# Big-head attention on one core: accumulators over three banks, queries in the score ring, diagonal subtractions on GpSimd

## The reference, cut to what matters

```python
qkv = jnp.einsum('bnc,fc->bnf', xn, w_qkv)                 # 8 heads x 128
q = q * scale_attn
sim = jnp.einsum('bihd,bjhd->bhij', q, k)
sim = jnp.where(causal_mask, neg, sim)
attn = jax.nn.softmax(sim, axis=-1)
out = jnp.einsum('bhij,bjhd->bihd', attn, v)
out = jnp.einsum('bnf,cf->bnc', out.reshape(b, n, 1024), w_out)
x = _layernorm(x + out)                                    # then the next block's own norm
```

## Time and profile before

| | |
|---|---|
| median of 3 runs | 2038.41 us (2037.45 to 2038.93) |
| profiled execution, its own time | 2044.93 us |
| span from its first to its last instruction | 2043.2 us |
| TensorE busy, share of the span | 1804.0 us, 88% |
| VectorE busy | 1570.7 us, 77% |
| ScalarE busy | 1374.6 us, 67% |
| GpSimd busy | 423.4 us, 21% |
| mean granted TensorE clock | 0.925 |

### The profile page before, as it was taken

The page is one execution under the profiler, slowest core; times in us unless marked ns, Lnnn a source line. Parts: engine busy times, 40 slices in busy tenths (PEclk is TensorE's granted clock), DMA queues, the critical chain, the costliest instruction groups (busy, mean ns, idle before and its releaser), DMA issues. The chain is left out here.

```text
span 2043.2 us, 40577 instructions
## 1 busy us (share of the span) xinstructions
PE 1804.0 (88%) x15880; PEld 967.7 (47%) x15880; DVE 1570.7 (77%) x2299; ACT 1374.6 (67%) x2569; POOL 423.4 (21%) x650
## 2 busy tenths in 40 slices
PE   6799999999999798669889998989678999999784
PEld 2122222222223388536778887978512322233384
DVE  5899999999997443457878788877578979886534
ACT  3499999999999543246555556565347898888431
POOL 4201000000002314323332221222231101122413
PEclk8599999999999989879999999989867999999698
DMA  5000000000000268400000000000100000000274
GB/s 168 1 3 3 4 11 4 5 9 4 7 8 7 96 226 297 154 4 1 1 1 1 1 1 1 1 1 1 54 0 2 4 4 12 5 12 6 60 263 153
DMA packets 52879, 81.57 MB, mean 40 GB/s; under 512 B 9200, under 2 KB 37744, under 8 KB 52560
## 3 DMA queue, kind: packets, MB, share of 16 engines
q1 hardware_dynamic: 47520, 70.50, 10.8%
q0 software_dynamic: 3072, 6.30, 1.0%
q10 hardware_dynamic: 2096, 2.17, 0.4%
HBM read 64.13 MB, written 12.06 MB: 37 GB/s over the span
## 5 line engine op out<-in xcount | busy, mean ns | idle before, releaser
L827 DVE TENSOR_REDUCE a_mx<-psum 128x2 f32<-128x1024 f32 (+2 forms) x832 | 906.3, 1156 | 77.0 <-PE psum L602 42.2
L753 ACT ACTIVATE a_cs<-psum 128x512 f32<-128x512 f32 (+3 forms) x1664 | 857.0, 572 | 78.6 <-PE psum L620 60.1
L643 PE MATMUL psum<-a_cs,a_V 128*16 128x256 f32 (+1 forms) x6400 | 501.6, 385 | 20.8 <-ACT a_OD L733 9.7
L602 PE MATMUL psum<-a_KS,a_QS 48*128 48x512 bf16 (+3 forms) x1664 | 330.2, 389 | 29.9 <-DVE a_mx L827 27.7
L620 PE MATMUL psum<-a_QS,a_KS 51*128 51x512 bf16 (+3 forms) x1664 | 336.7, 379 | 4.9 <-ACT a_cs L753 3.1
L2140 PE MATMUL psum<-b_VW,b_ST 128*128 128x129 f32 x2176 | 256.3, 279 | 21.1 <-DVE X L2265 21.1
L2140 PEld LDWEIGHTS psum<-b_VW,b_ST 128*128 128x128 f32 x2176 | 250.4, 195 | 23.1 <-DVE X L2265 23.1
L620 PEld LDWEIGHTS psum<-a_QS,a_KS 51*128 51x128 bf16 x1664 | 87.8, 93 | 354.4 <-ACT a_cs L753 310.3
L643 PEld LDWEIGHTS psum<-a_cs,a_V 128*16 128x16 f32 x6400 | 107.5, 94 | 244.2 <-issue 120.3
L2240 DVE TENSOR_TENSOR b_M<-b_M,b_ST 128x512 f32<-128x512 f32 (+3 forms) x288 | 174.8, 607 | 37.6 <-ACT b_ST L2179 6.7
L2186 ACT ACTIVATE b_ST<-b_ST 128x2048 f32<-128x2048 f32 x48 | 91.9, 1914 | 153.3 <-DVE b_ST L2248 153.3
(11 more groups left out here) (232 smaller groups left out, 1776.7 us busy)
## 6 DMA issues: line engine op xcount, KB each, us to landing
e_W<-in_l_experts SPq DMA_DIRECT2D x45, 576.0 KB, 5.5
e_W<-in_l_experts SPq DMA_DIRECT2D x21, 768.0 KB, 5.8
yg<-e_yout SPq DMA_DIRECT2D x14, 256.0 KB, 5.8
xg<-zeros SPq DMA_DIRECT2D x2, 1472.0 KB, 10.1
a_cs<-in_rope ACTq DMA_DIRECT2D x4, 512.0 KB, 10.5
a_QS<-a_mrow SPq DMA_DIRECT2D x128, 3.0 KB
a_cs<-in_rope SPq DMA_DIRECT2D x1, 2048.0 KB, 8.1
a_num<-a_OD SPq DMA_DIRECT2D x120, 16.0 KB
```

The costliest lines, as they stand in the source:

```text
L602: mm = pe.matmul(ps[:, 2 * slot + half, 0:width], QS[rows, 2 * p + i, q_cols(qb, qt * P, P)], KS[rows, 2 * p + i, c * BLK:c * BLK + width] ...
L643: mm = pe.matmul(ps[32 * j:32 * j + 2 * HD, AV_BANK, a:b], V[:, kt, HPP * p + j, :], probs(e, a, b), start=(kt == 0 and half == 0), stop=last,
L753: act.activation(probs(HPP * s + j, c, BLK), ps[:, plan.bank(entry), c:BLK], ACT.Exp, scale=scale).then_inc(exp_done, 1)
L827: dve.tensor_reduce(mx[:, pk % 2, qt, 2 * i:2 * i + 2, c], banks, AX.X, ALU.max).then_inc(max_done, 1)
```

## The change

Four things change in `big_head_attention` and its planner.

The two accumulators take turns over three banks (5, 6 and 7), so a product waits for the accumulation three halves back instead of two. Value products use three banks as well. Queries and folds lose their own bank and take their places in the ring of the five score banks, in the order in which TensorE makes queries, scores and folds. The four diagonal subtractions of an atom move from VectorE to GpSimd, into its list at the event `subtract`. The early folds, and the third `normalize`, are placed later on the plan's clock.

```diff
@@ KeyPlan.turn
-                self.norms += [(self.clock + 0.5 + n, ("measure", g, behind)), (self.clock + 12.0 + 2 * n + 2 * (n // 2), ("normalize", g)),
-                               (self.clock + 17.0 + 3 * n, ("fold", g))]
+                self.norms += [(self.clock + 0.5 + n, ("measure", g, behind)), (self.clock + (12.0, 14.0, 47.0)[n], ("normalize", g)),
+                               (self.clock + (45.0, 48.0, 54.0)[n], ("fold", g))]
@@ KeyPlan.lay
+        self.ring = [event for event in self.events if event[0] in ("query", "score", "fold")]
+        self.place_of = {event: n for n, event in enumerate(self.ring)}
@@ big_head_attention
-    S_BANKS, G_BANK, O_BANK = 5, 5, 6
+    RING, O_BANK, O_BANKS = 5, 5, 3
...
+        def o_bank(a, half):
+            return O_BANK + (2 * a + half) % O_BANKS
+        def bank_of(event):
+            return plan.place_of[event] % RING
+        def wait_bank(eng, event):
+            n = plan.place_of[event] - RING
+            if n < 0:
+                return
+            what, of = plan.ring[n][:2]
+            if what == "query":
+                eng.wait_ge(g_done, of + 1)
+            elif what == "fold":
+                eng.wait_ge(norm.h_ready, early[of] + 1)
+            else:
+                eng.wait_ge(copied, plan.tile0[of] + plan.ring[n][2] + 1)
@@ gpsimd
+                def subtract(a):
+                    pool.wait_ge(row_done, a + 1)
+                    for i in range(TPB):
+                        one = tile(a, TPB * plan.atoms[a][0] + i)
+                        pool.tensor_tensor(one, one, row[:, a % 2, i * P:], ALU.subtract).then_inc(diag_sub, 1)
...
+                    elif event[0] == "subtract":
+                        subtract(event[1])
@@ tensor, product
-                        elif a:
-                            pe.wait_ge(added, 2 * a - 1 + half)
+                        elif 2 * a + half >= O_BANKS:
+                            pe.wait_ge(added, 2 * a + half - O_BANKS + 1)
@@ vector, subtract
-                    for i in range(TPB):
-                        one = tile(a, TPB * qb + i)
-                        dve.tensor_tensor(one, one, row[:, a % 2, i * P:], ALU.subtract).then_inc(diag_sub, 1)
```

More of the change, by code:

```diff
@@ L2039, in v_bank @@
         def v_bank(n):
-            return O_BANK + n % 2
+            return O_BANK + n % O_BANKS
+        def o_bank(a, half):
[13 more added lines that the diff above has]
+                eng.wait_ge(copied, plan.tile0[of] + plan.ring[n][2] + 1)
         def x_cols(g):
@@ L2083, in _ @@
             def _(pe):
-                asked, folded = [0], [0]
                 def fold(g):
[L2087 to L2091, removed]
+                    wait_bank(pe, ("fold", g))
+                    norm.transpose(pe, early[g], bank_of(("fold", g)))
                 def query(a):
                     qb, h = plan.atoms[a]
[L2095 to L2100, removed]
+                    wait_bank(pe, ("query", a))
+                    pe.matmul(ps[:, bank_of(("query", a)), :], A[:, h, :], xnT[:, qb * BLK:(qb + 1) * BLK],
                               start=True, stop=True).then_inc(g_ready, 1)
@@ L2104, in value @@
                     n = 2 * t + c
-                    if n >= 2:
-                        pe.wait_ge(v_a if n % 2 == 0 else v_d, n // 2)
+                    if n >= O_BANKS:
+                        pe.wait_ge((v_a, v_d)[(n - O_BANKS) % 2], (n - O_BANKS) // 2 + 1)
                     pe.matmul(ps[:, v_bank(n), :], xnT[:, t * P:(t + 1) * P],
@@ L2111, in score @@
                 def score(a, kt):
-                    n, c = plan.tile0[a] + kt, plan.first_col(a, kt)
+                    c = plan.first_col(a, kt)
                     if kt == 0:
@@ L2116, in score @@
                         pe.wait_ge(x_low, kt // TPB + 1)
-                    if n >= S_BANKS:
-                        pe.wait_ge(copied, n - S_BANKS + 1)
-                    keys, out_ = slice(kt * P, (kt + 1) * P), ps[:, n % S_BANKS, c:BLK]
+                    wait_bank(pe, ("score", a, kt))
+                    keys, out_ = slice(kt * P, (kt + 1) * P), ps[:, bank_of(("score", a, kt)), c:BLK]
                     pe.matmul(out_, xL[:, keys], GH[:, a % 2, c:BLK], start=True, stop=False)
@@ L2139, in product @@
                         cols = slice((i % 2) * W, (i % 2 + 1) * W)
-                        mm = pe.matmul(ps[:, O_BANK + half, cols], ST[:, plan.at[a][kt // TPB], kt % TPB, i * P:(i + 1) * P],
+                        mm = pe.matmul(ps[:, o_bank(a, half), cols], ST[:, plan.at[a][kt // TPB], kt % TPB, i * P:(i + 1) * P],
                                        VW[:, kt, h, :], start=(kt == 0 and i % 2 == 0), stop=(kt == TPB * qb + i),
@@ L2163, in query @@
                         act.wait_ge(s_ready, plan.tile0[a - 1])
-                    act.activation(GH[:, a % 2, :], ps[:, G_BANK, :], ACT.Copy).then_inc(g_high, 1)
+                    act.activation(GH[:, a % 2, :], ps[:, bank_of(("query", a)), :], ACT.Copy).then_inc(g_high, 1)
                 def split(g):
@@ L2178, in score @@
                         act.wait_ge(av_done, 2 * (plan.before[a] + 1))
-                    act.activation(tile(a, kt), ps[:, n % S_BANKS, c:BLK], ACT.Copy).then_inc(copied, 1)
+                    act.activation(tile(a, kt), ps[:, bank_of(("score", a, kt)), c:BLK], ACT.Copy).then_inc(copied, 1)
                 def exponentials(a):
@@ L2204, in _ @@
                     elif event[0] == "fold":
-                        norm.store(act, early[event[1]], event[1], G_BANK)
+                        norm.store(act, early[event[1]], event[1], bank_of(event))
                         norm.keep(act, early[event[1]], event[1])
@@ L2213, in query @@
                     dve.wait_ge(g_high, a + 1)
-                    dve.tensor_tensor(GL[:, a % 2, :], ps[:, G_BANK, :], GH[:, a % 2, :].bitcast(F32),
+                    dve.tensor_tensor(GL[:, a % 2, :], ps[:, bank_of(("query", a)), :], GH[:, a % 2, :].bitcast(F32),
                                       ALU.subtract).then_inc(g_done, 1)
@@ L2259, in accumulate @@
                     mine = rec[:, a % 2, 2 * half:2 * half + 2]
-                    sums = ps[:, O_BANK + half, 0:2 * W].rearrange("p (i n) -> p i n", n=W)[:, :, P:W]
+                    sums = ps[:, o_bank(a, half), 0:2 * W].rearrange("p (i n) -> p i n", n=W)[:, :, P:W]
                     dve.reciprocal(mine.rearrange("p (i o) -> p i o", o=1), sums).then_inc(inverted, 1)
@@ L2264, in accumulate @@
                         t = TPB * qb + 2 * half + i
-                        ins = dve.scalar_tensor_tensor(out=X[:, t, :], in0=ps[:, O_BANK + half, i * W:i * W + P],
+                        ins = dve.scalar_tensor_tensor(out=X[:, t, :], in0=ps[:, o_bank(a, half), i * W:i * W + P],
                                                        scalar=mine[:, i:i + 1], in1=X[:, t, :], op0=ALU.mult, op1=ALU.add)
```

## The result

The changed kernel takes **2248.91 us** (median of 4 runs, 2246.83 to 2251.89) where the kernel before took 2037.93 on the same chip (4 runs, 2035.38 to 2038.93): a ratio of 1.1038, 95% interval 1.1019 to 1.1058. It is 10% slower; forecast were 2226 us and a range of 2170 to 2295. The profiled execution took 2247.01 us with a span of 2245.2, GpSimd's busy time went from 423.4 to 510.0 us, VectorE's from 1570.7 to 1516.9, and the mean granted clock from 0.925 to 0.888.

The account below looks back on a forecast made before the run. The stage was taken as a loop through ScalarE, VectorE and GpSimd, lengthened by GpSimd's reconfigurations: 50 + 29 + 57 + 31 + 20 - 6 - 3 + 10 = +188 on 2044.9, 2233, less 6.5: 2226 us, range 2170 to 2295.

Parts of the forecast that it names:

- atoms 0, 1, 2 and 15: Single atoms: 13.6 us for atom 15, 7 each for atoms 1 and 2, 3 for atom 0; together +31.
- six pairs: Pairs of atoms in blocks 1 and 0: a round of 29.0 us instead of 19.5, +9.5 each, +57.
- block 2: Rounds of atoms 17 to 23: 26.4 us instead of 19.29, +7.1 each, +50; nothing counted for atom 16.
- block 3 without 27, and the folds: Seven rounds of 28.8 us instead of 24.68, +29; moved folds end TensorE's 7.6 us stall, less 2: -6.
- atom 27: Subtractions queued behind the powers and `call` reduction: 30.1 us from its reduction to its exponentials instead of 13.4; +20.
- TensorE's clock: Longer idle in block 2 lowers the granted clock, slowing score tiles; VectorE's chain hides most: +10, bounds 0 and 40.
- T: GpSimd's reconfiguration from a reduction to a tensor_tensor, ahead of the subtractions: 6.7 to 6.9 us, taken as 6.9.
- R: GpSimd's reconfiguration from a tensor_tensor back to a reduction, behind the masks: 5.6 to 5.9 us, taken as 5.9.
- R without cover: Rival: reconfiguration issued only after the instruction's own wait, so short idle times don't hide it: +36, 2262 us; chance 0.11.
- the ring: Queries among the score banks let TensorE run four tiles ahead, not five: nothing, or 0.7 us a round without cover.
- the prediction's own sign of being wrong: The forecast is wrong if something else, such as TensorE at half clock, makes rounds longer than 30 us.
- The blocking rival: Rival: reconfigurations cost nothing, but GpSimd's and VectorE's subtractions block each other: +28 less 22, 2044 us; chance 0.04.

Follow-up runs that it names:

- e3: The changed kernel with the subtractions back on VectorE and, in their place on GpSimd, a tiny multiplication nobody reads; 2144.98 us, ratio 1.0497 to before.
- e4: The changed kernel with one more all-reduce, of a buffer nobody reads, directly behind each run of subtractions on GpSimd; 2175.19 us, ratio 1.0653 to before.
- e1: The changed kernel with only the diagonal subtractions put back on VectorE; 2029.17 us, ratio 0.9929 to before.
- e7: The changed kernel with extra matmuls ahead of each fourth score tile in blocks 2 and 3, keeping TensorE busy; 2235.15 us, ratio 1.0951 to before.
- e2: The kernel before with only the diagonal subtractions moved to GpSimd; 2250.77 us, ratio 1.1018 to before.
- e8: The kernel before with only the early blocks' folds placed late as in the changed kernel; ratio 0.9987 to before.
- e10: The changed kernel with the diagonal subtractions back on VectorE and the early folds at their old place; ratio 0.9919 to before.
- e5: The changed kernel with every all-reduce of the stage replaced by a multiplication of the same columns; 2056.77 us, ratio 1.0077 to before.
- e6: The changed kernel with the subtractions back on VectorE and every all-reduce of the stage replaced by a multiplication; 2020.99 us, ratio 0.9910 to before.

## Why the prediction was right, step by step

The forecast was 2226 and the time 2248.91. The cause was right, and one term of the sum was too small: what a late restart of TensorE does to the rounds of blocks 2 and 3. By the stage it was +188 against +206.5 (763.8 - 557.3):

| step of the sum | predicted | measured |
|---|---|---|
| atoms 0, 1, 2 and 15 | +31 | +31.7 |
| six pairs | +57 | +55.5 |
| block 2 (measured with atom 16) | +50 | +60.7 |
| block 3 without 27, and the folds | +29 - 6 | +41.0 |
| atom 27 | +20 | +22.1 |
| third bank (the stage's end) | -3 | -4.6 |
| TensorE's clock | +10 | within the rounds |

- **Reconfigurations.** Right in number (with the powers, the `call` and the stage's start the 54 are all there), place and size: T was taken as 6.9 and is 7.0 on the mean of 26, R as 5.9 and is 6.0 of 19. e3 and e4 show the reading behind it, that only what stands on the loop counts: the same number of them costs some 78 us less when the way back moves under the copies. In the pair shown above the chain holds step by step: from the round's start at 1013.75 the subtractions were put at 21.8 to 28.7 us and stand at 22.3 to 28.9. For atoms 1 and 2 the prediction took half of a bound, 7 each, without a row for it; they took 8.1 and 7.6, and that the guess came so near is luck. The Trainium skill's figure for a first call ("GPSIMD Engine Reference", Instruction dispatch: about 6 us, with no instruction shown) agrees with R (6.0 us); T (7.0) is 1 us longer than it. Here every switch pays, also one back to what ran before.
- **R without cover** (the rival of 2262) is refuted. In the round shown above the masks end at 1272.35, and the reduction starts 5.84 later; its reconfiguration stands at 1272.5, while VectorE's maximum runs until 1273.12 (line 2087's sequencer row, from 1260 to 1290):

```profile
L2087 POOLq MODIFY_POOL_CONFIG  x2: 6/6/6, 1272.5 to 1272.6; - x2
```

- **The subtractions** were taken as 3.45 us an atom; the fences show 3.30 to 3.36. Atom 27 was given 30.1 us from its reduction's end to its exponentials' and took 29.2, in the timelines of GpSimd and ScalarE (of the earlier trace rows the same piece is 13.4):

```profile
1487.47 1.80 POOL L2087 PARTITION_ALL_REDUCE b_row<-b_M  x1 [6.45 <-issue]
1496.77 4.91 POOL L1826 TENSOR_TENSOR b1n_scales<-b1n_both,b1n_half 128x8 f32<-128x8 f32 x3 [7.50 <-issue]
1507.68 0.39 POOL L2106 PARTITION_ALL_REDUCE b_call<-b_call  x1 [6.01 <-issue]
1514.81 3.30 POOL L2093 TENSOR_TENSOR b_ST<-b_ST,b_row 128x512 f32<-128x512 f32 x4 [6.74 <-issue]
...
1517.74 0.72 ACT L2209 ACTIVATE b_ST<-b_ST 128x256 f32<-128x256 f32 x2 [0.16 <-POOL b_ST L2093]
```

- **TensorE's clock and the ring: the term that was too small.** "VectorE's chain hides most; I add 10", and for the ring "nothing": VectorE's maximum did cover the score tiles before, but now R starts at the masks' end, and the masks need the last copies. The prediction let the masks end 8.06 and 10.45 us into a round; they end at 9.5 and 12.6. Against the single rounds that the prediction read, and over seven rounds each, that is 1.45 x 7 + 2.17 x 7 = 25 us, of which 10 were in the sum. The split can be had in two ways. With the clock up and queries in the ring the masks end at 8.7 and 11.2 to 11.3 (most rounds of e1, those of e7 in which the clock stays up): 0.8 and 1.3 earlier than in the changed kernel, so the clock is 0.8 x 7 + 1.3 x 7 = 15 us and the ring the other 10. With the clock down and queries apart (e2) they end at 9.0 and 11.9: by this the clock is 16 and the ring 9. The ring's share can be seen where TensorE starts again, in the changed kernel and then in e2, in rounds that begin at 1261.76 and 1262.54:

```profile
1263.11 0.77 PE L2139 MATMUL psum<-b_GH,b_xL 128*128 128x512 f32 x1 [8.34 <-DVE b_GL L2233]
```

```profile
1263.56 0.79 PE L2128 MATMUL psum<-b_GH,b_xL 128*128 128x512 f32 x1 [7.50 <-ACT b_ST L2187]
```

With the query in the ring TensorE waits for VectorE's low part of it, 1.35 us into the round; without, for the first score copy, 1.02. The ring's bound in the prediction, 0.7 a round if its cover were gone, was that price; what was wrong was to count the cover on after R had taken it away. With this the prediction's own sign of being wrong, rounds longer than 30 us with TensorE at half clock, came true in block 3 (30.9 on the mean). It explains some 2.1 us of that round; the rest of what it grew by is the predicted 4.1, and in e4, with the way back moved, the round is 25.7.
- **Folds and third bank.** The folds were given 6 and are worth 3 (e8) or nothing that can be told (e10); the third bank was given 3 and is worth 7 when VectorE does the subtractions (some of the -4.6 at the stage's end is what it gives here). Neither term decides anything here.
- **What was missed, 18.5 us.** Against the mean rounds of the kernel before, the rounds grew by 8.2 and 6.4 us instead of 7.1 and 4.1. With the prediction's rounding that is 23 us more over seven each; less the 10 in the sum, 13. Atom 16, counted as nothing, took 3.0 more. The folds give some 3.5 instead of 6 (atoms 28 and 29 together grew by 9.3 us, two mean rounds by 12.7), and the other steps leave -0.3.
- **The range.** Its lower end was added up wrong: 13, 17 and 10 off 2226 is 2186, not 2180. Nothing hangs on it.
- **The blocking rival** was right as a mechanism and wrong in what it would give. It was priced at +28 less the gains, 2044; e5 against e6 has +35.8, in the pairs too (1.8 us each, where a gain of 2 had been counted). The Trainium skill has the rule ("SBUF — State Buffer", SBUF: two separate sides): the port pair that both engines share is held for a whole instruction. The stretched rows of both engines (1608 ns against 850, 2946 against 2286) agree with it. Even free of reconfigurations, the moved subtractions would have cost more than the other edits give.

## What to carry to other kernels

Idle time of an engine says nothing about what an instruction costs there: look at what stands next to it in that engine's list. Here one cheap tensor_tensor between two partition reductions on GpSimd pays a switch on either side (7.0 and 6.0 us), and the loop pays for the side that nothing covers. When the loop gets a hole, ask what the hole does to TensorE's clock: here the next tiles came at half speed (granted clock 0.50) just where they were waited for. And take a change apart before dropping it: three of these four edits together made the kernel 0.7% faster, where all four made it 10% slower.

## What was not expected of the hardware

- The masks (TENSOR_SCALAR_AFFINE_SELECT) run on either side of a switch without one: in e4 they follow a reduction, in the changed kernel the subtractions, each time with no "issue" ahead of them and no MODIFY_POOL_CONFIG at their line.
- T varies from 6.7 to 7.7 us in one program, the changed kernel, and R from 5.7 to 6.5.
- In the two rounds of e7 shown the granted clock stayed at 1.00 behind 1.30 us of idle and fell behind 2.20, and extra matmuls without use made the program faster.
- Beside VectorE's wide subtractions GpSimd's took 1608 ns instead of 850.
